# The opening of the shared experts: order of TensorE's steps, of GpSimd's gathers and of ScalarE's casts

## The chip, the cores and the metric

The kernel runs on one core of a Trainium2 chip. The metric is the device time of one execution in microseconds (us), as the median of several runs. Inside the core, TensorE (PE) multiplies matrices, VectorE (DVE), ScalarE (ACT) and GpSimd (POOL) work on tiles of 128 rows, SyncE (SP) issues transfers, and the engines run side by side and wait for each other through semaphores only.

## The reference, cut to what matters

The program is two blocks of cross-attention and mixture of experts over `x` of 4 x 512 tokens with 512 features. The change lies where block 0 ends and the feed-forward part of block 1 begins. What is computed there:

```
x = x + tanh(g_ffn[0]) * mixture0(layernorm(x))            # 2 of 8 experts per token
# block 1, attention: one summary row per batch element
x = x + tanh(g_xattn[1]) * (layernorm(layernorm(x) + summary) * gamma + beta)
# block 1, feed-forward: on flat = layernorm(x)
h   = silu(flat @ Sg) * (flat @ Su)                        # 2 shared experts, 512 wide each
out = h @ Sd  +  4 of 64 routed experts per token
x = x + tanh(g_ffn[1]) * out
```

## The kernel before, in words

The kernel is a sequence of blocks: attention of block 0, `mixture0` (8 experts), `middle` (the end of mixture 0, attention of block 1, routing, and the shared experts), `experts` (64 routed experts) and `finish`. Tokens are handled as 16 tiles of 128; each batch element is a group of four tiles. `middle` is written out by hand: each engine has its own list of steps, executed strictly in the order in which they stand. The change is in the opening of `middle`, the work on group 0 (tiles 0 to 3) before TensorE can start on the shared experts.

For each tile of group 0, in this order:

- GpSimd **gathers** two expert rows per token by indirect DMA into `y0` (`gather(0, ...)`, line 1226), two gathers a tile, eight in all.
- ScalarE makes two diagonal matrices of mixing weights (`diagonals`, 1428).
- TensorE sums `x` and the two weighted rows into a PSUM bank (`mixed(j)`, 1304 and 1306: three 128x512 fp32 products). The banks are `pU[0], pU[1], pC, pU[0]`, so tile 3 has the bank of tile 0, and `mixed(3)` waits for `x3_ready` of tile 0.
- TensorE spreads the summary row of each batch element over 128 rows (`summary_row(b)`, 1295), and ScalarE copies it from its bank (`summary_rows`, 1435). The four rows use banks that the transposes and the first chunks need later, so `transposed(0, 0)` waits for all four copies.
- VectorE takes statistics of the bank, GpSimd raises the variance to the power -1/2 (`inverse_std`, 1215), VectorE makes `z` from the bank (`mix_in`, 1639) and signals `y_made`; statistics of `z` follow, and `z` is scaled by gamma (`attend_to`, 1651).
- TensorE adds the scaled beta into the same bank (`with_beta(j)`, 1314), after `y_made`; VectorE then forms the new `x` from `z` and that bank (`take_in`, 1660), which waits for `with_beta`. Statistics again, and `lnf` holds scale and bias of the last layernorm.
- ScalarE writes the normalised tile (`flat_tile`, 1439), TensorE transposes it (1324), ScalarE copies the transpose twice (`turn`, 1445 and 1446), VectorE takes the low part (`keep`, 1623, signal `fT_kept`), and TensorE starts the shared experts' first products (`shared.up`, 2079) when tiles 0 and 1 are kept. Tiles 2 and 3 go the same way behind them.

Weights are split into a high and a low part. ScalarE casts a half of a weight to the high part (`first_part`, 1418, 128x2048), VectorE subtracts to get the low part (`split`, 1182). `SPLITS` lists four such pieces: two of the up weights `Su`, in SBUF since `mixture0`, and two of the gate weights `Sg`, which SP loads (line 1799) when tile 1's gathers have landed. Two splits stand on VectorE's list inside `mix_in(0)`, the third between `take_in(0)` and `keep(0)`, the fourth after `mix_in(2)`.

GpSimd's list begins with one iota and three memsets (`power` is an operand of `inverse_std`; the others are used later by routing), a drain, a wait for the zeroed tables, and the eight gathers.

The lists of TensorE and ScalarE at this place, before the change:

```
summary_row(0); mixed(0); mixed(1); summary_row(1); mixed(2)
summary_row(2); summary_row(3); with_beta(0); with_beta(1)
mixed(3); transposed(0, 0); transposed(0, 1)
---
summary_rows(range(B)); act.wait_ge(gate_loaded, 16 * NSH)
first_part(SPLITS[NSH:]); flat_tile(0, 0..1); turn(0, 0..1)
```

Of the kernel before, what the change touches and what calls it, by code (L numbers as in the profile page):

```python
# [14 lines left out]
P = 128  # L15
B, SEQ, D = 4, 512, 512
TILES = B * SEQ // P
TPB = SEQ // P
DB = D // P
# [3 lines left out]
NSH, HSH = 2, 512  # L23
# [1037 lines left out]
def middle(nc, A, T):  # L1061
# [4 lines left out]
    with c:  # L1066
# [30 lines left out]
        ve, power = sb("ve1", [P, TPB]), sb("power", [P, TPB])  # L1097
# [105 lines left out]

        @block.gpsimd
        def _(pool):
            nc.gpsimd.iota(tokens[:], [[P, TILES]], base=0, channel_multiplier=1)
            nc.gpsimd.memset(T["stage_all"][:, NSH * DB * HSH:], 0.0)
            nc.gpsimd.memset(power[:], -0.5)
            nc.gpsimd.memset(chosen[:], 0.0)
            pool.drain()  # L1210

            def inverse_std(k, a=0, z_=TPB):

                pool.wait_ge(var_ready, k + 1)
                nc.gpsimd.tensor_tensor(rstd[:, a:z_], ve[:, a:z_], power[:, a:z_], ALU.pow).then_inc(rstd_ready, 1)

            pool.wait_ge(T["s_zero1"], 16 * (ZERO_CHUNKS + SUMS * E0 + 1))
            def gather(n, tiles):

                for j in tiles:  # L1220
                    if n == 1:
                        pool.wait_ge(x2_full, j + 1)
                    elif n > 1:
                        pool.wait_ge(x2_ready, TPB * (n - 2) + j + 1)
                    for k in range(2):
                        nc.gpsimd.indirect_dma_start(
                            y0[:, j, k, :], None, T["ytab0"],
                            bass.IndirectOffsetOnAxis(take0[:, n * TPB + j, k:k + 1], 0)).then_inc(gathered[j], 16)

            def dispatch(g, tiles):  # L1230
                pool.wait_ge(slot_ready, g + 1)
                for j in tiles:
                    for k in range(TOP1):

                        nc.gpsimd.indirect_dma_start(  # L1235
                            T["tab1"], bass.IndirectOffsetOnAxis(slot1[:, j, k:k + 1], 0), flat[:, j, :], None,
                            bounds_check=E1 * CAP1 - 1, oob_is_err=False).then_inc(scattered, 16)

            def sum_up(n):

                inverse_std(stat(n - 1, 0))
                for j in range(TPB):
                    if n == 1 and j == 0:
                        pool.wait_ge(summary_ready, B)
                    pool.wait_ge(z_ready, (n - 1) * TPB + j + 1)
                    nc.gpsimd.tensor_tensor(z[:, j, :], z[:, j, :], summary[:, n, :], ALU.add).then_inc(y_ready, 1)
                for j in range(TPB):
                    nc.gpsimd.tensor_tensor(x_sb[:, n * TPB + j, :], x_sb[:, n * TPB + j, :], beta[:],
                                            ALU.add).then_inc(xb_ready, 1)
                inverse_std(stat(n - 1, 1))  # L1250

            def keep_low(n):

                inverse_std(stat(n - 1, 2))
                for j in range(TPB):

                    pool.wait_ge(fT_ready, TPB * n + j + 1)
                    cols = slice(j * P, j * P + P)
                    nc.gpsimd.tensor_tensor(flat_lo[:, :, cols], flatTt[:, j], flat_hi[:, :, cols],
                                            ALU.subtract).then_inc(fT_kept, 1)  # L1260

            gather(0, range(TPB))
            for k in range(3):
                inverse_std(first_stat(0, k), 0, 2)
            gather(1, (0, 1))
            inverse_std(first_stat(2, 0), 2, 4)
            gather(1, (2,))
            inverse_std(first_stat(2, 1), 2, 4)
            gather(1, (3,))
            inverse_std(first_stat(2, 2), 2, 4)  # L1270
            pool.wait_ge(beta_ready, 1)
            sum_up(1)
            dispatch(0, range(TPB))
            keep_low(1)
            for n in range(2, B):
                gather(n, range(TPB))
                dispatch(n - 1, (0, 1))
                sum_up(n)
                dispatch(n - 1, (2, 3))
                keep_low(n)  # L1280
            dispatch(B - 1, range(TPB))
            pool.wait_ge(scattered, 16 * TILES * TOP1)

        @block.tensor
        def _(pe):
# [5 lines left out]
            def summary_row(b):  # L1291

                if b == 0:
                    pe.wait_ge(srow_ready, 1)
                nc.tensor.matmul(row_bank[b][:], ident[0:B, b:b + 1].broadcast_to([B, P]), srow,
                                 start=True, stop=True).then_inc(rows_full, 1)

            def mixed(j):

                pe.wait_ge(diag_ready, j + 1)  # L1300
                pe.wait_ge(gathered[j], 16 * 2)
                if j == 3:
                    pe.wait_ge(x3_ready, 1)
                nc.tensor.matmul(x2_bank[j][:], ident[:], x_sb[:, j, :], start=True, stop=False)
                for k in range(2):
                    last = nc.tensor.matmul(x2_bank[j][:], diag[:, 2 * j + k, :], y0[:, j, k, :], start=False, stop=(k == 1))
                last.then_inc(x2_full, 1)

            def with_beta(j):

                pe.wait_ge(y_made, j + 1)
                if j == 0:
                    pe.wait_ge(beta_ready, 1)
                nc.tensor.matmul(x2_bank[j][:], ident[:], beta[:], start=False, stop=True,
                                 skip_group_check=True).then_inc(x2b_full, 1)
# [32 lines left out]

            def first_steps():

                summary_row(0)
                mixed(0)
                mixed(1)
                summary_row(1)
                mixed(2)
                summary_row(2)
                summary_row(3)
                with_beta(0)
                with_beta(1)
                mixed(3)  # L1360
                pe.wait_ge(small_loaded, 80)
                transposed(0, 0)
                transposed(0, 1)
# [43 lines left out]
        def _(act):  # L1407
# [23 lines left out]
            def summary_rows(bs):  # L1431

                for b in bs:
                    act.wait_ge(rows_full, b + 1)
                    nc.scalar.copy(summary[:, b, :], row_bank[b][:]).then_inc(summary_ready, 1)
# [17 lines left out]
            first_part(SPLITS[1:2])  # L1453
            diagonals(2)
            diagonals(3)
            summary_rows(range(B))
            act.wait_ge(gate_loaded, 16 * NSH)
            first_part(SPLITS[NSH:])
            for j in range(2):
                act.wait_ge(lnf_ready, j + 1)  # L1460
                flat_tile(0, j)
            for j in range(2):
                turn(0, j)

            def step(g):
                for half, cols in halves(g):
# [677 lines left out]
```

## Time and profile before

| | us |
|---|---|
| median of 3 runs | 1182.45 |
| the 3 runs | 1184.02, 1178.94, 1182.45 |
| the profiled execution, its own time | 1178.42 |
| its span | 1176.7 |
| TensorE busy in the span | 1045.8 (89%) |
| VectorE, ScalarE, GpSimd busy | 675.2, 480.4, 552.2 |

The span is the time between the first and the last recorded instruction; the profiled execution took 1.7 us more than its span. `middle` starts at 550.2 us of the span. A line of a timeline gives the start, the duration, the engine, the source line, the operation and its tiles, how many instructions were merged, and in brackets how long the engine had idled before and what ended that. PSUM tiles are all called `bank`. `w_sd` is also the memory of the diagonals and of the summary row, `stage_up` that of `z` and of the transposed tiles, so these names stand in the rows for them. A 128x512 fp32 product leaves two records.

### The profile page before, as it was taken

The numbers are of one execution on the slowest core, as the hardware profiler recorded it, in microseconds if no ns is written. First come the engines' busy times: TensorE is split into PE (matmuls) and PEld (weight loads), VectorE is DVE, ScalarE is ACT, GpSimd is POOL, SyncE is SP. The second block draws the span as 40 slices with busy tenths as digits, with TensorE's granted clock in tenths as the row PEclk, the third lists the DMA queues.
The fourth block names the chain that finished last, engine by engine and source line by source line (L and its number), as shares of the span: only waits on it lengthen the run. The fifth ranks groups of instructions, "written<-read, shape, count | busy, mean of one in ns | idle before, by whom it ended". The sixth has DMA issues, their size and how long they took to land. (4 is left out here: it accounts for less than half of the span.)

```text
span 1176.7 us, 18454 instructions
## 1 busy us (share of the span) xinstructions
PE 1045.8 (89%) x5324; PEld 735.5 (63%) x5324; DVE 675.2 (57%) x1558; ACT 480.4 (41%) x835; POOL 552.2 (47%) x517
## 2 busy tenths in 40 slices
PE   3999999999879999997798799999998999999920
PEld 2555555555437777774498377586687777787710
DVE  4677777776458888884677256265312333343426
ACT  2465565564338888886322121222212222222200
POOL 4344544644426666666415557446151344333530
PEclk9999999999989999998899899999998999999965
DMA  9976555773534333333610131130029999999639
GB/s 294 345 235 204 169 181 203 252 252 99 197 134 168 103 105 107 107 108 105 217 34 27 75 102 37 41 122 13 27 83 328 362 342 301 279 323 344 146 89 361
DMA packets 133243, 206.54 MB, mean 176 GB/s; under 512 B 36743, under 2 KB 44935, under 8 KB 133178
## 3 DMA queue, kind: packets, MB, share of 16 engines
q1 hardware_dynamic: 113274, 172.72, 43.4%
q0 software_dynamic: 19616, 32.50, 10.1%
q8 instruction: 32, 0.52, 0.2%
q10 hardware_dynamic: 288, 0.52, 0.1%
q14 instruction: 33, 0.27, 0.1%
HBM read 137.56 MB, written 87.03 MB: 191 GB/s over the span
## 5 line engine op out<-in xcount | busy, mean ns | idle before, releaser
L1922 POOL DMA_INDIRECT sums<-summary,m_token x64 | 99.2, 1550 | 161.2 <-DVE summary L1996 86.2
L906 POOL TENSOR_TENSOR m_down_lo<-wo,m_down_hi 128x512 fp32r<-128x512 f32 x80 | 133.0, 1682 | 79.7 <-ACT m_down_hi L1001 79.7
L514 PE MATMUL bank<-win,vT 128*128 128x512 f32 x256 | 124.2, 598 | 0.0
L604 ACT ACTIVATE win<-bank 128x512 f32<-128x512 f32 x128 | 69.5, 595 | 109.4 <-PE bank L506 109.2
L674 DVE TENSOR_REDUCE negmax<-bank 128x1 bf16<-128x512 f32 x128 | 87.0, 679 | 43.3 <-PE bank L521 43.0
L1015 DVE TENSOR_TENSOR m_up_lo<-w,m_up_hi 128x1024 fp32r<-128x1024 f32 x80 | 98.3, 1230 | 12.0 <-ACT m_up_hi L973 10.9
L521 PE MATMUL bank<-k_hi,q_parts 128*128 128x512 f32 x128 | 76.8, 600 | 17.0 <-DVE negmax L674 13.4
L1945 PE MATMUL bank<-y,m_w 128*128 128x128 f32 x736 | 89.7, 275 | 0.0
L1235 POOL DMA_INDIRECT tab<-stage_up,slot x64 | 66.3, 1036 | 49.2 <-DVE slot L1570 31.0
L1945 PEld LDWEIGHTS bank<-y,m_w 128*128 128x128 f32 x736 | 86.4, 193 | 0.5 <-issue 0.5
L2100 PE MATMUL bank<-w_sd,stage_gate 128*128 128x512 f32 x192 | 84.9, 598 | 0.3 <-DVE stage_gate L2090 0.3
L2086 ACT ACTIVATE sh_gate_a<-bank 128x512 f32<-128x512 f32 (+1 forms) x40 | 20.5, 513 | 149.9 <-PE bank L2079 149.9
L1970 ACT COPY y<-bank 128x512 f32<-128x512 f32 x64 | 37.5, 586 | 102.5 <-PE bank L1937 99.4
L1996 DVE TENSOR_SCALAR summary<-bank,m_weight 128x512 f32<-128x512 f32 x64 | 48.1, 751 | 54.2 <-DMA sums<-summary,m_token 29.5
L2079 PE MATMUL bank<-flat_hi,w_hi 128*128 128x512 f32 (+1 forms) x320 | 74.8, 357 | 3.0 <-DVE flat_lo L1623 1.9
L404 POOL DMA_INDIRECT tab<-xn,slot x32 | 32.8, 1024 | 94.4 <-DVE slot L708 89.5
L2079 PE MATMUL bank<-flat_lo,w_hi 128*128 128x512 f32 (+1 forms) x320 | 73.0, 351 | 0.0
L2079 PE MATMUL bank<-flat_hi,w_lo 128*128 128x512 f32 (+1 forms) x320 | 72.4, 349 | 0.0
L927 PE MATMUL bank<-m_up_hi,m_xT_hi 128*128 128x512 f32 x160 | 69.6, 435 | 1.9 <-DVE m_up_lo L1015 1.6
L1983 DVE TENSOR_TENSOR m_gh<-m_gh,bank 128x128 f32<-128x128 f32 x64 | 18.4, 287 | 90.0 <-ACT m_gh L1974 90.0
L514 PEld LDWEIGHTS bank<-win,vT 128*128 128x128 f32 x256 | 47.0, 190 | 26.1 <-issue 15.3
L2100 PEld LDWEIGHTS bank<-w_sd,stage_gate 128*128 128x128 f32 x192 | 36.4, 193 | 42.8 <-issue 42.6
(282 smaller groups left out, 2383.8 us busy)
## 6 DMA issues: line engine op xcount, KB each, us to landing
tab<-zeros SPq DMA_DIRECT2D x16, 1056.0 KB
m_w<-in_L_ffn_Wg SPq DMA_DIRECT2D x46, 256.0 KB, 5.3
m_w<-in_L_ffn_Wu SPq DMA_DIRECT2D x46, 256.0 KB, 5.9
m_w<-in_L_ffn_Wd SPq DMA_DIRECT2D x46, 256.0 KB, 6.2
m_x<-tab SPq DMA_DIRECT2D x40, 256.0 KB, 2.6
ytab<-m_y SPq DMA_DIRECT2D x40, 256.0 KB, 2.0
stage_up<-tab SPq DMA_DIRECT2D x32, 264.0 KB, 7.4
m_x<-tab SPq DMA_DIRECT2D x32, 264.0 KB, 5.7
```

Source lines behind the costliest of these rows:

```text
L514: nc.tensor.matmul(pO[s * 2 + h][:], vT[:, s, sb_, h:h + 2, :].rearrange("p a c -> p (a c)"), probs[:, sb_ % 2, h, :], start=(sb_ == 0), s ...
L521: nc.tensor.matmul(pM[:], q_parts[:, s, h, t * P:t * P + P], k_hi[:, s, h, :], start=True, stop=True).then_inc(pm_full, 1)
L604: nc.scalar.activation(probs[:, b % 2, h, :], pS[h][:], ACT.Exp, scale=1.0 / HEAD).then_inc(p_ready, 1)
L674: nc.vector.tensor_reduce(negmax[:, s, m:m + 1], pM[:], AX.X, ALU.max, negate=True).then_inc(pm_read, 1)
L906: nc.gpsimd.tensor_tensor(dn_lo[:, m, :], row(wo0, e * MB + m), dn_hi[:, m, :], ALU.subtract).then_inc(dn_lo_ready, 1)
L927: last = nc.tensor.matmul(pH[s][:], x[:, s, d, :], w[:, d, :], start=(d == 0 and part == 0), stop=(d == DB - 1 and part == 2))
L1015: nc.vector.tensor_tensor(up_lo[:, at, :], blocks(w01, e * DB + half * HALF, HALF), up_hi[:, at, :], ALU.subtract).then_inc(up_lo_ready, 1)
L1235: nc.gpsimd.indirect_dma_start(T["tab1"], bass.IndirectOffsetOnAxis(slot1[:, j, k:k + 1], 0), flat[:, j, :], None, bounds_check=E1 * CAP1 ...
L1922: nc.gpsimd.indirect_dma_start(T["sums1"][e % SUMS], bass.IndirectOffsetOnAxis(token[:, e % META:e % META + 1], 0), y[:, e % RING, :], Non ...
L1945: last = nc.tensor.matmul(pH[s][:, k * CAP1:(k + 1) * CAP1], w[:, b, :], xT[:, s, b, :], start=(b == 0), stop=(b == DB - 1))
L2079: last = nc.tensor.matmul(out, w[:, k, s, wc], x[:, d, cols], start=(d == 0 and part == 0), stop=(d == DB - 1 and part == 2))
L2100: last = nc.tensor.matmul(pY[j][:], self.h[:, n, j * P:j * P + P], sd[:, s, b, :], start=(n == 0), stop=(n == self.CHUNKS - 1))
```

## The change

TensorE's list: `mixed(0)` goes before `summary_row(0)`, and `with_beta(0)` and `with_beta(1)` go before `mixed(2)`. GpSimd's list: the iota, the memsets and their drain go behind the eight gathers of group 0. ScalarE's list: the first gate cast goes between the copies of summary rows 0 and 1 and those of rows 2 and 3; the second gate cast goes behind both turns.

```diff
         @block.gpsimd
-            nc.gpsimd.iota(tokens[:], [[P, TILES]], base=0, channel_multiplier=1)
-            nc.gpsimd.memset(T["stage_all"][:, NSH * DB * HSH:], 0.0)
-            nc.gpsimd.memset(power[:], -0.5)
-            nc.gpsimd.memset(chosen[:], 0.0)
-            pool.drain()
...
             gather(0, range(TPB))
+            nc.gpsimd.memset(power[:], -0.5)
+            nc.gpsimd.iota(tokens[:], [[P, TILES]], base=0, channel_multiplier=1)
+            nc.gpsimd.memset(T["stage_all"][:, NSH * DB * HSH:], 0.0)
+            nc.gpsimd.memset(chosen[:], 0.0)
+            pool.drain()
             for k in range(3):
                 inverse_std(first_stat(0, k), 0, 2)
...
             def first_steps():
+                mixed(0)
                 summary_row(0)
-                mixed(0)
                 mixed(1)
                 summary_row(1)
+                with_beta(0)
+                with_beta(1)
                 mixed(2)
                 summary_row(2)
                 summary_row(3)
-                with_beta(0)
-                with_beta(1)
                 mixed(3)
...
-            summary_rows(range(B))
+            summary_rows(range(2))
             act.wait_ge(gate_loaded, 16 * NSH)
-            first_part(SPLITS[NSH:])
+            first_part(SPLITS[NSH:NSH + 1])
+            summary_rows(range(2, B))
             for j in range(2):
                 act.wait_ge(lnf_ready, j + 1)
                 flat_tile(0, j)
             for j in range(2):
                 turn(0, j)
+            first_part(SPLITS[NSH + 1:])
```

## Rows read from the trace of the kernel before

**Rows 1.** Busy time by stretch: length, PE, PEld, DVE, ACT, POOL, clock, DMA share, GB/s

```profile
548.00:584.00 36.00, 26.00 (x54) 9.15 (x55) 20.64 (x38) 18.26 (x25) 17.61 (x19) 0.83 0.57 187
```

**Rows 2.** Timeline of PE, 556 to 584 us: start, duration, instruction [idle before]

```profile
556.88 1.12 PE L1295 MATMUL bank<-w_sd,ident 4*128 4x512 f32 x2 [1.45 <-DVE w_sd L1515]
557.93 1.12 PE L1304 MATMUL bank<-x_sb,ident 128*128 128x512 f32 x2
...
560.61 1.02 PE L1304 MATMUL bank<-x_sb,ident 128*128 128x512 f32 x2
...
563.27 1.12 PE L1295 MATMUL bank<-w_sd,ident 4*128 4x512 f32 x2
566.85 1.80 PE L1304 MATMUL bank<-x_sb,ident 128*128 128x512 f32 x2 [2.45 <-DMA y<-ytab,take]
...
571.29 1.98 PE L1295 MATMUL bank<-w_sd,ident 4*128 4x512 f32 x4
573.20 1.98 PE L1314 MATMUL bank<-beta,ident 128*128 128x512 f32 x4
...
579.90 1.63 PE L1324 MATMUL bank<-ident,stage_up 128*128 128x128 f32 x8 [1.83 <-issue]
583.42 1.22 PE L2079 MATMUL bank<-flat_hi,w_hi 128*128 128x256 f32 x4 [1.89 <-DVE flat_lo L1623]
```

**Rows 3.** Timeline of DVE, 557 to 583 us

```profile
557.42 2.29 DVE L1182 TENSOR_TENSOR w_lo<-stage_up,w_hi 128x2048 fp32r<-128x2048 f32 x1 [0.20 <-DMA y<-ytab,take]
560.81 0.70 DVE L1635 BATCH_NORM_STATS2 bn<-bank 128x6 f32<-128x512 f32 x1 [1.09 <-PE bank L1306]
561.42 2.28 DVE L1182 TENSOR_TENSOR w_lo<-stage_up,w_hi 128x2048 fp32r<-128x2048 f32 x1
563.61 0.69 DVE L1635 BATCH_NORM_STATS2 bn<-bank 128x6 f32<-128x512 f32 x1
...
565.73 1.41 DVE L1639 SCALAR_TENSOR_TENSOR stage_up<-bank,rstd,summary 128x512 f32<-128x512 f32 x2 [0.85 <-POOL rstd L1215]
...
570.04 1.41 DVE L1651 SCALAR_TENSOR_TENSOR stage_up<-stage_up,mv,gamma 128x512 f32<-128x512 f32 x2
574.36 1.61 DVE L1660 SCALAR_TENSOR_TENSOR x_sb<-stage_up,rstd,bank 128x512 f32<-128x512 f32 x2 [2.92 <-PE bank L1314]
...
578.87 2.31 DVE L1182 TENSOR_TENSOR w_lo<-stage_gate,w_hi 128x2048 fp32r<-128x2048 f32 x1
581.67 0.69 DVE L1623 TENSOR_TENSOR flat_lo<-stage_up,flat_hi 128x512 fp32r<-128x512 f32 x1 [0.49 <-ACT stage_up L1446]
```

**Rows 4.** Timeline of POOL, 550 to 565 us

```profile
550.48 0.15 POOL L1209 MEMSET chosen<- 128x64 bf16 x1
551.51 1.00 POOL L1226 DMA_INDIRECT y<-ytab,take  x1 [0.88 <-issue]
...
558.35 2.19 POOL L1226 DMA_INDIRECT y<-ytab,take  x1 [0.30 <-issue]
...
562.10 2.42 POOL L1226 DMA_INDIRECT y<-ytab,take  x1 [0.30 <-issue]
564.96 0.73 POOL L1215 TENSOR_TENSOR rstd<-ve,power 128x2 f32<-128x2 f32 x1 [0.43 <-DVE ve L1587]
```

**Rows 5.** Timeline of ACT, 573 to 589 us

```profile
573.78 3.70 ACT L1418 CAST w_hi<-stage_gate 128x2048 fp32r<-128x2048 f32 x2
578.99 1.52 ACT L1439 ACTIVATE stage_up<-x_sb,lnf 128x512 f32<-128x512 f32 x2 [1.50 <-DVE lnf L1667]
588.42 0.38 ACT L2086 ACTIVATE sh_gate_a<-bank 128x256 f32<-128x256 f32 x1 [4.48 <-PE bank L2079]
```

**Rows 6.** Busy time in half microseconds: where the granted clock fell and rose

```profile
567.00:567.50 0.50, 0.50 (x1) 0.12 (x2) 0.41 (x2) 0.00 (x0) 0.00 (x0) 0.60 1.03 397
...
570.50:571.00 0.50, 0.50 (x2) 0.00 (x0) 0.50 (x2) 0.00 (x0) 0.00 (x0) 0.98 0.00 0
```

**Rows 7.** Timeline of PE, first product that waits inside the chunks

```profile
599.85 0.74 PE L2079 MATMUL bank<-flat_hi,w_hi 128*128 128x256 f32 x4 [1.12 <-DVE stage_gate L2090]
```

## The prediction

> **What bounds the kernel now.** I read the busy time by stretch first, then the timelines of the four engines over the opening of `middle`, then the clock. In the 36 us around the opening TensorE is busy 26.0, VectorE 20.6, ScalarE 18.3 and GpSimd 17.6 [rows 1]: no engine fills it, so a chain of dependencies sets its length, and the end to look for is the first product of the shared experts at 583.42, which waits for VectorE's `keep` [rows 2]. Followed back from there: `keep(0)` at 581.67 waits for ScalarE's `turn` [rows 3]; ScalarE starts the flat tiles at 578.99 after 1.50 idle, for `lnf` [rows 5]; `lnf` comes from `take_in(0)`, which started at 574.36 after 2.92 us in which VectorE had nothing but TensorE's `with_beta` to wait for [rows 3]. `with_beta` ran at 573.20 although its `z` was there since about 567.1 (565.73 + 1.41), because `mixed(2)` (from 566.85, after 2.45 idle for tile 2's gather) and rows 2 and 3 (from 571.29) stood ahead of it on TensorE's list [rows 2, 3]. Before that the chain is: the second statistics at 563.61, GpSimd's power at 564.96, `z` at 565.73, `attend_to` at 570.04 to 571.45 [rows 3, 4].
>
> From `keep` on VectorE works nearly without a gap, and the first product that waits in the chunks, at 599.85, waits again for VectorE [rows 7]. So what counts is how far `keep(0)` moves; a faster TensorE in chunk 0 would not. Nothing after the opening is timed against anything but these signals: the loads of expert weights, routing and the later groups all wait for products of this chain, so I carry the move to the end one for one. That is the main assumption.
>
> **The parts of the change.**
>
> *with_beta ahead of mixed(2).* Removed: VectorE's wait of 2.92. `attend_to(0)` ends at 571.45; with a gap of 0.1 as between its neighbours `take_in(0)` starts at 571.55 instead of 574.36: 2.8 us gained. `with_beta(0)` can start when the first `z` is written, about 566.45, and costs at full clock half of the pair's pitch (573.20 to 575.25, cut by `mixed(3)`: 2.05), 1.0, or 2.0 at half clock: done by 568.5, 3.0 us before it is needed. The new wait is TensorE's, for `y_made`; behind it stand `mixed(2)`, rows 2 and 3, `mixed(3)`, and the transposes. What is late next is this queue. From 566.45: with_beta pair 2.05, `mixed(2)` 2.66 (pitch 560.61 to 563.27), rows 2 and 3 1.91 (571.29 to 573.20), `mixed(3)` 2.82 (the end of the idle at 579.90 less 1.83 is 578.07, less the pair's end at 575.25) [rows 2]: 9.44, so ready for the transposes at 575.9. At the moved time the first flat tile is written at 578.99 + 0.76 - 2.8 = 576.95 [rows 5]: TensorE is there 1.0 earlier, if its clock stays up. The bank of `mixed(3)` is free when `take_in` of tile 0 is through, about 572.4, and `mixed(3)` comes at 573.1.
>
> *The clock.* The granted clock fell 0.3 us after the idle of 2.45 before `mixed(2)`, and was back at 570.5 after 3.4 us of dense work [rows 6]; 0.50 is 1.2 GHz, 1.00 is 2.4. That made `mixed(2)` last 4.44 (566.85 to 571.29) instead of 2.66: 1.8 us. In the changed kernel TensorE idles from about 564.3 to 566.45, 2.1 us, so the same fall is likely, now in `with_beta` and `mixed(2)`. Then the queue ends at 577.7, 0.75 after the first flat tile. In the old order the turn began at 580.5, when the two flat tiles were written (578.99 + 1.52) and about 0.6 after the transposes began; at the moved times ScalarE is free at 577.7 and TensorE's first transposed tile is there at 577.7 + 0.8 (half of 1.63) = 578.5 [rows 2, 5]. Cost between 0 (no fall) and 0.8; I take 0.5, nearer the upper end, since shorter idles, 1.83 and 1.89 in a row, also left TensorE slow: four products of 256 columns took 1.22 at 583.42 and 0.74 at 599.85 [rows 2, 7].
>
> *mixed(0) ahead of summary_row(0).* Tile 0's bank is full 1.05 earlier (the pitch of row 0, 556.88 to 557.93), so the first statistics start at about 559.8, not 560.81 after 1.09 idle, and the second split ends at about 562.6 [rows 2, 3]. But the second statistics need `mixed(1)`, and the sum of TensorE's work before it is the same, so it starts at 563.4 instead of 563.61: 0.2 gained. More only if TensorE can start before 556.88, that is if tile 0's gathers, which released VectorE at 557.42 [rows 3], land earlier.
>
> *Gathers first.* The first gather started at 551.51 after 0.88 idle, of which 0.30 stands before every gather; the iota and the memsets began 0.2 before 550.48 [rows 4]. So it moves up by 0.3 to 1.0. With it tile 0 lands by 556.4 to 557.0, and TensorE starts up to 0.5 earlier. Against this, the five instructions and the drain (at most 0.37 + 0.58) now stand between the last gather and GpSimd's first power, which had 0.43 idle before it [rows 4]. And the gathers do not simply shift. Those at 558.35 and 562.10 took 2.19 and 2.42 instead of 1.00; both began inside a split on VectorE (557.42 to 559.71, 561.42 to 563.70) and ended 0.83 and 0.82 after it [rows 3, 4]. The new second split runs from about 560.4 to 562.6. If two gathers are left at that time, the last ends at 564.6 and the power starts at 565.0 to 565.6, as late as 0.6 after the old time; if one is left, it ends at 563.4 and the power starts when the variance is there, 0.2 to 0.7 earlier. Range -0.6 to +0.7; I take 0.
>
> On this the Trainium skill (SBUF — State Buffer, "SBUF: two separate sides") has a rule that speaks against the change: a VectorE instruction with two SBUF inputs and a GpSimd instruction that reads SBUF exclude each other for their whole length, and a locked-out GpSimd cannot write descriptors. The stretched gathers of this trace agree. By the rule alone the early gathers win nothing once the splits begin; by the rows alone the same, which is why the step is put at 0.
>
> *The gate cast split in two.* The casts ran at 573.78, behind row 3's copy, 1.88 each, 3.70 together [rows 5]. The weights had landed by 570.5, where the DMA share is 0.00 [rows 6]. Now the first cast runs at about 570 to 572, ahead of rows 2 and 3, which TensorE fills at 571.1 to 574.8; the copies, 0.6 each, are done by 575.5, before `lnf` at 576.2: nothing lost. The second cast, 1.9, goes behind the turns, from about 580 to 582; its reader is the fourth split, some 5 us after `keep(1)`, and the first silu, which had 4.48 idle before 588.42 [rows 5], covers it and the table load. Cost 0; without that cover 1.9. The third split on VectorE, 2.31 from `lnf`, ends before the turn as now (581.18 against 581.67) [rows 3].
>
> **Sum.** 2.8 + 0 - 0.5 = 2.3 us earlier `keep`. The profiled execution took 1178.42: it would take 1176.1. It is 4.0 under the median of the three runs; the four executions together average 1180.95. From that average the forecast is 1178.7, which I take; it is 3.8 under the median shown, of which 1.5 is spread between executions.
>
> **Rivals.**
>
> *The clock stays up, or an earlier start comes through.* 2.8 + 0.7 and, where a slow stretch elsewhere in the chunks falls differently, up to 1.8 more: 3.5 to 5.3, about 1176. For it: the idle shrinks from 2.45 to 2.1. Against: the idles of 1.83 and 1.89 that were enough once [rows 2]. 0.17.
>
> *The gain is given back.* The gathers and memsets make the power late by 0.6, TensorE's queue costs 0.8, and the end of `middle` is held by something that does not move: 0 to 1.4 left, about 1180.5. For it: the lock on gathers; against: the signals below all come from this chain. 0.25.
>
> *TensorE's queue takes the place of the wait, slower.* If the clock fell at 566.5 and stayed at 1.2 GHz to the transposes, the queue of 9.44 would take near 18 us and end at 584: 4 us after the old 579.90, so 3 to 4 us slower, about 1184. It decides from the point where the low clock lasts over 4 us beyond the 3.4 seen (each us of it costs half a us; the queue's end passes 579.90). Against: the clock came back under the same products [rows 6]. 0.05. The ScalarE copy of this mechanism, rows 2 and 3 and the flat tiles behind a late load of `Sg`, needs a landing 6 us later than in this trace; in the 0.05.
>
> *The change does not do what it says:* `take_in` would still wait for `with_beta`. Excluded by the 3.0 us in hand unless `z` itself is late; in the second rival.
>
> **How the numbers follow.** Forecast (gain 1.5 to 3.5) 0.53; the rivals 0.17, 0.25, 0.05. Range: gains from -1.5 to 5.3 and a spread of the median of +-2 around the average: 1174.5 to 1184. 0.5% (5.9 us) is about what a measurement of this kernel tells from no change. A forecast of 1178.7 lies inside 1176.5 to 1188.4; with the spread a fifth of the forecast and half of the first rival come out under 1176.5, and a little of the rest: 0.23 faster. The third rival's tail gives 0.04 slower. 0.73 remain.
>
> **What would show it.** In the changed trace: `take_in` with next to no idle before it; `with_beta` some 7 us earlier; `keep(0)` about 2.3 earlier against the start of `middle`; the power after the eighth gather with less than 0.43 idle; the clock low within `with_beta` and `mixed(2)`; the copies of rows 2 and 3 done before `lnf`. Wrong would be: transposes that wait for `mixed(3)` by over 1 us, a fourth split that waits for its cast, or chunk times that shift by another amount than `keep`.

## The result, and the profile after

The changed kernel took 1185.0 us, median of 22 runs (1181.8 to 1189.2); the kernel before, run beside it, 1181.5, median of 22 (1176.4 to 1189.2). The ratio is 1.0032 with a 95% interval of 1.0019 to 1.0045: 3.8 us slower (2.2 to 5.3). 2.3 us faster was forecast.

The profiled execution of the changed kernel had a span of 1185.0. Its opening began 3.7 us later than that of before, in code that both kernels share, so all positions below count from **the opening's start**, the first state product of TensorE (550.27 in before, 553.99 here). From there `keep(0)` comes at 34.3 instead of 31.4: 2.9 later.

The timeline of GpSimd in the changed kernel, the last three of the eight gathers, a memset behind them, and the first power:

```profile
561.00 3.99 POOL L1220 DMA_INDIRECT y<-ytab,take  x1 [0.30 <-issue]
565.29 2.86 POOL L1220 DMA_INDIRECT y<-ytab,take  x1 [0.30 <-issue]
568.46 0.95 POOL L1220 DMA_INDIRECT y<-ytab,take  x1 [0.30 <-issue]
...
569.63 0.17 POOL L1260 MEMSET chosen<- 128x64 bf16 x1
573.15 0.73 POOL L1209 TENSOR_TENSOR rstd<-ve,power 128x2 f32<-128x2 f32 x1 [3.35 <-issue]
```

The drain is an instruction of GpSimd's queue; the view by its source line gives its length and its start:

```profile
L1261 POOLq DRAIN  x1: 15104/15104/15104, 557.9 to 557.9; - x1
```

It entered at 557.9, while gathers were still being issued, and ended at 573.0, 3.2 us after the last memset. The power followed 0.15 later. In before the idle ahead of this power was 0.43, for the variance [rows 4]. What moved in the core's DMA engines meanwhile, in the view of busy time by stretch (the last three columns are the granted clock, the DMA share and GB/s):

```profile
571.00:572.00 1.00, 0.00 (x0) 0.00 (x0) 0.00 (x0) 0.59 (x1) 0.00 (x0) 1.00 0.80 324
572.00:573.00 1.00, 0.00 (x0) 0.00 (x0) 0.00 (x0) 1.00 (x1) 0.00 (x0) 1.00 0.04 16
```

In the view of the DMA queues the last packet of the gathers' queue falls before 572.4, and that of the queue of `Sg` before 571.2. So the drain's end lies 0.6 behind the end of the gathers' transfers. VectorE, with the lines that answer to [rows 3]:

```profile
564.45 0.70 DVE L1636 BATCH_NORM_STATS2 bn<-bank 128x6 f32<-128x512 f32 x1 [0.28 <-PE bank L1305]
...
568.27 0.70 DVE L1636 BATCH_NORM_STATS2 bn<-bank 128x6 f32<-128x512 f32 x1 [0.93 <-PE bank L1305]
...
573.92 1.41 DVE L1640 SCALAR_TENSOR_TENSOR stage_up<-bank,rstd,summary 128x512 f32<-128x512 f32 x2 [4.37 <-POOL rstd L1209]
...
579.71 1.41 DVE L1661 SCALAR_TENSOR_TENSOR x_sb<-stage_up,rstd,bank 128x512 f32<-128x512 f32 x2
...
588.25 0.69 DVE L1624 TENSOR_TENSOR flat_lo<-stage_up,flat_hi 128x512 fp32r<-128x512 f32 x1 [1.93 <-ACT stage_up L1445]
```

`take_in(0)` no longer waits, as forecast, but `z` waits 4.37 for the power. TensorE, against [rows 2]:

```profile
561.60 1.10 PE L1303 MATMUL bank<-x_sb,ident 128*128 128x512 f32 x2 [1.18 <-DMA y<-ytab,take]
...
574.73 3.78 PE L1313 MATMUL bank<-beta,ident 128*128 128x512 f32 x4 [5.44 <-DVE stage_up L1640]
578.30 1.92 PE L1303 MATMUL bank<-x_sb,ident 128*128 128x512 f32 x2
...
581.92 1.98 PE L1294 MATMUL bank<-w_sd,ident 4*128 4x512 f32 x4
...
586.51 1.04 PE L1323 MATMUL bank<-ident,stage_up 128*128 128x128 f32 x8
```

It idled 5.44 for `z`, ran the pair at a granted clock of 0.50, 1.2 GHz (3.78, not 1.98), and reached the transposes at 586.5, 2.1 after the first flat tile was begun. ScalarE, against [rows 5]:

```profile
584.42 1.52 ACT L1438 ACTIVATE stage_up<-x_sb,lnf 128x512 f32<-128x512 f32 x2
587.15 0.58 ACT L1444 CAST flat_hi<-bank 128x512 fp32r<-128x512 f32 x1 [1.21 <-PE bank L1323]
```

The turn waited 1.21 for them.

Against before, the 2.9 at `keep(0)` add up so: the power is 4.5 later, 1.0 of it because the variance was and 3.5 by the drain; 2.8 come back from the wait for `with_beta` that is gone, and 0.2 because `take_in` took 1.41 and not 1.61; ScalarE starts the flat tile 0.3 later behind `lnf`, since it still copies row 3; the turn's wait adds 1.15.

### The profile page after: what moved, and what is told of

It is laid out like the page before. It is cut to its first block and busy times, and to the rows that moved or that the text cites. A ratio compares the mean times of both kernels' runs of the same rounds, so it can differ in the third digit from the quotient of the medians.

```text
span 1185.0 us, 18454 instructions
## 1 busy us (share of the span) xinstructions
PE 1053.3 (89%) x5324; PEld 738.7 (62%) x5324; DVE 675.7 (57%) x1558; ACT 480.1 (41%) x835; POOL 553.0 (47%) x517
## 5 line engine op out<-in xcount | busy, mean ns | idle before, releaser
L521 PE MATMUL bank<-k_hi,q_parts 128*128 128x512 f32 x128 | 76.5, 598 | 18.2 <-DVE negmax L674 14.2
L404 POOL DMA_INDIRECT tab<-xn,slot x32 | 32.7, 1023 | 96.0 <-DVE slot L708 91.1
L521 PEld LDWEIGHTS bank<-k_hi,q_parts 128*128 128x128 f32 x128 | 25.0, 195 | 62.3 <-DVE negmax L674 50.5
```

Of the source, the lines that this page charges most:

```text
L521: nc.tensor.matmul(pM[:], q_parts[:, s, h, t * P:t * P + P], k_hi[:, s, h, :], start=True, stop=True).then_inc(pm_full, 1)
```

## The experiments

Times are positions from the opening's start in each kernel's own profiled execution; ratios are to the kernel before on the same chip. In the table "first of TensorE" is the step that stands first, row 0 or `mixed(0)`, and "2nd st." the second tile's statistics. A profiled execution is one of those timed, and not the median one: of `power first` the second time, `power by VectorE` and `power first, row first` it was the slowest of the twelve.

| kernel | first of TensorE | 2nd st. | power | take_in(0) | keep(0) | ratio (95%) |
|---|---|---|---|---|---|---|
| before, four profiles | row | 13.3, 13.5, 16.3, 17.6 | 14.7, 14.9, 17.7, 19.0 | 24.1, 24.1, 24.2, 25.5 | 31.4, 31.4, 31.3, 32.6 | 1 |
| changed, two profiles | mixed | 14.3, 14.0 | 19.2, 19.1 | 25.7, 25.7 | 34.3, 34.5 | 1.0032 (1.0019 to 1.0045) |
| gathers back | mixed | 14.6 | 15.9 | 22.5 | 29.7 | 0.9988 (0.9969 to 1.0006) |
| gathers only | row | 16.3 | 19.1 | 25.6 | 32.7 | 1.0012 (0.9995 to 1.0030) |
| drain late | mixed | 13.8 | 19.0 | 25.6 | 33.0 | 1.0016 (0.9999 to 1.0033) |
| power first | mixed | 14.4, 13.9 | 15.8, 15.3 | 22.3, 21.8 | 29.5, 30.6 | 0.9969 (0.9950 to 0.9988), 0.9986 (0.9965 to 1.0007) |
| gathers only, Sg late | row | 18.2 | 19.5 | 26.1 | 33.2 | 1.0026 (1.0003 to 1.0049) |
| power first, row first | row | 18.9 | 20.2 | 26.8 | 34.3 | 1.0017 (1.0000 to 1.0034) |
| beta only | row | 16.6 | 17.9 | 24.5 | 34.5 | 1.0004 (0.9983 to 1.0025) |
| power first, casts back | mixed | 14.4 | 15.8 | 22.3 | 32.3 | 0.9999 (0.9980 to 1.0018) |
| power by VectorE | mixed | 14.2 | 15.5 | 22.1 | 29.6 | 0.9981 (0.9961 to 1.0001) |
| mixed first only | mixed | 14.6 | 15.9 | 22.5 | 29.6 | 0.9995 (0.9973 to 1.0017) |

**Which part of the change is it?** First GpSimd's list put back as it was, in the changed kernel (diff against the changed kernel):

```diff
+            nc.gpsimd.iota(tokens[:], [[P, TILES]], base=0, channel_multiplier=1)
+            nc.gpsimd.memset(T["stage_all"][:, NSH * DB * HSH:], 0.0)
+            nc.gpsimd.memset(power[:], -0.5)
+            nc.gpsimd.memset(chosen[:], 0.0)
+            pool.drain()
...
             gather(0, range(TPB))
-            nc.gpsimd.memset(power[:], -0.5)
-            nc.gpsimd.iota(tokens[:], [[P, TILES]], base=0, channel_multiplier=1)
-            nc.gpsimd.memset(T["stage_all"][:, NSH * DB * HSH:], 0.0)
-            nc.gpsimd.memset(chosen[:], 0.0)
-            pool.drain()
```

> The changed kernel with GpSimd's list as it was before: iota, memsets and drain ahead of the eight gathers. TensorE's and ScalarE's lists stay changed. Theory D (the drain behind the gathers does it): in the changed kernel GpSimd is idle 3.35 us between its last memset and the first power. Without that drain the power starts when the variance is there, at most 0.5 after it; take_in(0) starts with under 0.1 idle, some 22.9 us after the opening's start against 24.1 before and 25.7 changed; TensorE's queue costs 0.8 to 1.2 of the 2.8 won, so the kernel is 1.5 to 2 us faster than before (ratio 0.998 to 0.999). Rival Q (TensorE's new order does it: the queue behind with_beta and the low clock): the loss stays, ratio 1.002 to 1.004.

Measured 0.9988 (0.9969 to 1.0006), `keep(0)` at 29.7, and the power waits for nothing but the variance:

```profile
569.67 0.73 POOL L1215 TENSOR_TENSOR rstd<-ve,power 128x2 f32<-128x2 f32 x1 [3.76 <-DVE ve L1589]
```

Its interval and that of the changed kernel don't meet, and the two kernels differ in GpSimd's list alone. The loss sits there. Then that list alone, changed on the kernel before (the diff above, reversed):

> The kernel before with GpSimd's list alone changed (gathers first, then memsets, iota and drain). Theory D: the first power is some 4.4 us later against the opening's start; z, too; but with_beta had 2.9 us of wait behind mixed(2) to give, so take_in(0) and keep(0) come about 1.6 us later: ratio 1.001 to 1.002, and less slow than the changed kernel, since here mixed(2) and rows 2 and 3 run while z is late. Rival Q: GpSimd's change costs nothing: ratio 1.000, power with under 1 us of idle before it.

Measured 1.0012, the power at 19.1, as theory D said, with the idle below ahead of it; `keep(0)` at 32.7, against 31.3 to 32.6. Only the last 1.4 of the 6.15 are the drain's: the variance itself came at 17.6 here. The ratio's interval holds 1.

```profile
573.78 0.73 POOL L1209 TENSOR_TENSOR rstd<-ve,power 128x2 f32<-128x2 f32 x1 [6.15 <-issue]
```

**The drain, or what else moved?** TensorE's and ScalarE's lists changed, iota and memsets ahead of the gathers, only the drain behind (GpSimd's list, against before):

```diff
             nc.gpsimd.memset(chosen[:], 0.0)
-            pool.drain()
...
             gather(0, range(TPB))
+            pool.drain()
```

> TensorE's and ScalarE's lists changed; on GpSimd iota and memsets stay ahead of the gathers as before, and only the drain stands behind the gathers. Theory D: as slow as the changed kernel (ratio to before 1.002 to 1.004), idle of about 3 us before the first power, though no memset stands there. Rival M (the early gathers disturb the small loads, or the memsets behind the gathers take the time): as fast as the kernel with GpSimd's list back, 0.998 to 0.999.

Measured 1.0016, the power at 19.0, though the variance was there at 15.1:

```profile
571.47 0.73 POOL L1214 TENSOR_TENSOR rstd<-ve,power 128x2 f32<-128x2 f32 x1 [4.08 <-issue]
```

This kernel and `gathers back` differ in the drain's place alone and ran on the same chip: the power is at 19.0 and not at 15.9, `keep(0)` at 33.0 and not at 29.7, while their ratios' intervals overlap. The half of rival M about the memsets falls: none stands there. Its other half, the early gathers, falls with the next kernel, where they are as early (0.9) and the power waits for the variance alone. The other way round, the drain out of the way (against the changed kernel):

```diff
+            nc.gpsimd.memset(power[:], -0.5)
+            pool.drain()
...
             gather(0, range(TPB))
-            nc.gpsimd.memset(power[:], -0.5)
-            nc.gpsimd.iota(tokens[:], [[P, TILES]], base=0, channel_multiplier=1)
-            nc.gpsimd.memset(T["stage_all"][:, NSH * DB * HSH:], 0.0)
-            nc.gpsimd.memset(chosen[:], 0.0)
-            pool.drain()
             for k in range(3):
                 inverse_std(first_stat(0, k), 0, 2)
+            nc.gpsimd.iota(tokens[:], [[P, TILES]], base=0, channel_multiplier=1)
+            nc.gpsimd.memset(T["stage_all"][:, NSH * DB * HSH:], 0.0)
+            nc.gpsimd.memset(chosen[:], 0.0)
+            pool.drain()
```

> The changed kernel, but the memset of power and a drain stand ahead of the gathers, and the iota, the two other memsets and their drain behind the third inverse_std, when the eight gathers have landed some microseconds ago. Theory D with the drain waiting for landed transfers: the second drain takes under 0.6 us here, the first power waits for the variance alone, and the kernel is 1.5 to 2.5 us faster than before (0.998 to 0.999). If the drain costs a fixed 3.3 us after any gather, the first gathers of group 1 start over 3 us after the third power, which delays no chain at once but the power of tiles 2 and 3: ratio 1.001 or more. Rival Q: 1.002 to 1.004.

Measured 0.9969 (0.9950 to 0.9988): faster than before, and the fastest of the study. The second drain now stands 11 us behind the last gather's issue, with the DMA share at 0.00 from 580 to 583. It was 1.74 in the queue and ended 0.7 after the last memset, where under 0.6 was expected, and it left 1.47 idle ahead of the next gather, of which 0.30 stand there anyway. This costs a little: group 1's gathers now end so late that the power of tile 2 comes behind them, and `z` of tile 2 waits 1.42 for it, where it waits 0.84 with the gathers back.

```profile
571.47 0.73 POOL L1212 TENSOR_TENSOR rstd<-ve,power 128x2 f32<-128x2 f32 x1 [0.21 <-DVE ve L1590]
...
583.91 1.60 POOL L1223 DMA_INDIRECT y<-ytab,take  x1 [1.47 <-issue]
```

**What does the drain wait for?** Three kernels with it have the power at 19.0 to 19.2, whether the last gather ended at 15.4, 12.5 or 15.0. So it is no fixed time after the last gather's issue. `Sg` later, on the kernel with GpSimd's list alone changed:

```diff
-            sp.wait_ge(gathered[1], 16 * 2)
+            sp.wait_ge(gathered[3], 16 * 2)
             for s in range(NSH):
                 sp.dma_start(stage[0][:, s].rearrange("p (b h) -> p b h", b=DB),
```

> The kernel before with GpSimd's list changed (gathers, memsets, iota, drain), and SP's load of Sg moved behind the landing of tile 3's gathers instead of tile 1's. Theory L (the drain behind the gathers waits until what GpSimd has issued has landed, and the 2 MB of Sg in the same engines delay that): the last gathers land about 4 to 5 us after their start, at 16 to 17 us from the opening's start, and the first power starts within 1 us of that, 1.5 to 3 us earlier than the 19.0 seen in three kernels with this drain. Rival F (a fixed time of the drain after the gathers began, near 15 us from its entry into the queue): the power stays at 19.0. The gate casts come later than before by some 5 us, so the time itself need not improve: ratio 1.000 to 1.004.

The drain, and the stretches at its end (opening's start 553.42):

```profile
L1261 POOLq DRAIN  x1: 11816/11816/11816, 557.4 to 557.4; - x1
```

```profile
568.00:569.00 1.00, 1.00 (x2) 0.34 (x1) 0.32 (x1) 0.00 (x0) 0.00 (x0) 0.50 0.25 98
569.00:570.00 1.00, 1.00 (x3) 0.38 (x2) 1.00 (x2) 0.00 (x0) 0.00 (x0) 0.92 0.07 16
```

It ended at 569.2, which is 15.8 from the start, when the gathers had landed (SP issued `Sg` at 568.8, on tile 3's signal). It was 11.8 us in the queue instead of 15.0 to 15.1: rival F falls, theory L holds. The expectation was wrong in one point: the power still started at 19.5, because here the variance came that late. The time did not improve (1.0026).

A rival is left that was not on record: that the drain waits for every transfer of the core, those of `Sg` too. The trace of the kernel with the gathers only excludes it. Its drain:

```profile
L1261 POOLq DRAIN  x1: 15019/15019/15019, 558.7 to 558.7; - x1
```

It ended at 573.7. The DMA queues (packets, MB, share of 16 engines) from 572 to 573 and from 573 to 574; q0 is that of the gathers, which alone moved packets from 565 to 567.5 in the kernel with `Sg` late, when nothing else was under way:

```profile
q1 hardware_dynamic: 126, 0.24, 62.4%
q0 software_dynamic: 31, 0.07, 16.7%
...
q1 hardware_dynamic: 52, 0.09, 24.0%
```

From 573.0 on only the queue of `Sg` moved packets, until 574.2, and the drain ended amid them. In all five executions with a drain behind the gathers it ended 0.6 to 0.7 us after the last packet of the gathers' queue.

On the length of that landing the Trainium skill (DMA: Bandwidth & Descriptors, "Queues, rings and completion order") says that a DMA engine takes packets from its queues in turn. The runs agree: with `Sg` beside them the last gather needed about 7.4 us from its start to the drain's end (566.3 to 573.7, gathers only), without it 3.8 (565.4 to 569.2).

**Is mixed(0) ahead of row 0 worth anything?** Row 0 first again, in the kernel with power first:

```diff
-                mixed(0)
                 summary_row(0)
+                mixed(0)
```

> The kernel with power's memset and drain first, but summary_row(0) ahead of mixed(0) as before. Theory R (tile 0's gathers land after the summary row is ready, so the row filled the wait for them; mixed(0) first pushes the row between mixed(0) and mixed(1)): second statistics at 13.4 to 13.6 us from the opening's start against 14.4 to 14.6, everything after it 0.9 to 1.0 earlier, ratio 0.996. Rival (the gathers land first, the order does not matter, as the sum of the prediction had it): second statistics unchanged or 0.2 later, ratio 0.997.

Both expectations missed the size and the side: the second statistics moved from 14.4 to 18.9, not to 13.5, and the ratio from 0.9969 to 1.0017. TensorE:

```profile
562.80 1.84 PE L1296 MATMUL bank<-w_sd,ident 4*128 4x512 f32 x2 [2.41 <-DVE w_sd L1518]
564.57 2.08 PE L1305 MATMUL bank<-x_sb,ident 128*128 128x512 f32 x2
566.44 3.61 PE L1307 MATMUL bank<-y,w_sd 128*128 128x512 f32 x4
```

Row 0 waited for the summary row, which waited for the small loads, 2.2 us later here than in the profile of before (8.1 from the start, not 5.9). Behind that idle the granted clock fell: 0.54 from 563 to 564 and 0.50 (1.2 GHz) from 564 to 569, so most of row 0 and all of `mixed(0)` ran at 1.2 GHz. Over all profiles of the study the second statistics stand at 13.8 to 14.6 in the nine executions with `mixed(0)` first, and at 13.3 to 18.9 in the eight with row 0 first. Part of that spread is the small loads' own. Where VectorE took up the summary row at the same time, 7.1 to 7.2, they stand at 14.4 with `mixed(0)` first (`power first`, `casts back`) and at 16.3 with row 0 first (the third profile of before, `gathers only`). In the ratio the order's worth is less sure: 1.0017 (1.0000 to 1.0034) does not meet the first interval of `power first`, but it overlaps the second.

**with_beta alone**, on the kernel before:

```diff
                 summary_row(1)
+                with_beta(0)
+                with_beta(1)
                 mixed(2)
                 summary_row(2)
                 summary_row(3)
-                with_beta(0)
-                with_beta(1)
```

> The kernel before with one edit: with_beta(0) and with_beta(1) ahead of mixed(2). take_in(0) starts at about 21.3 us from the opening's start against 24.1. If the gate casts behind rows 2 and 3 (3.7 us on ScalarE) are what comes next, the rows are copied at 23.5 to 25.5, the casts end at 27.3 to 29.2, the flat tile starts there against 28.7 before: 1.4 earlier to 0.5 later, ratio 0.999 to 1.0005. If the casts do not matter, keep(0) is 2.3 earlier, ratio 0.998.

Measured 1.0004, `keep(0)` at 34.5, 1.9 to 3.2 us later than in the profiles of before. `take_in(0)` came at 24.5 and not at 21.3, because the second statistics stood at 16.6 in this execution, and the flat tile at 31.8, later than both branches had it. ScalarE:

```profile
582.41 0.59 ACT L1435 COPY summary<-bank 128x512 f32<-128x512 f32 x1 [0.27 <-PE bank L1295]
582.90 3.70 ACT L1418 CAST w_hi<-stage_gate 128x2048 fp32r<-128x2048 f32 x2
586.50 1.52 ACT L1439 ACTIVATE stage_up<-x_sb,lnf 128x512 f32<-128x512 f32 x2
```

`mixed(2)` and the rows are pushed back behind `with_beta`, the casts behind the rows with them, and the flat tile follows the casts without idle. The second branch of the expectation (casts do not matter) falls. The same from the other side, ScalarE's old list in the kernel with power first (against that kernel):

```diff
-            summary_rows(range(2))
+            summary_rows(range(B))
             act.wait_ge(gate_loaded, 16 * NSH)
-            first_part(SPLITS[NSH:NSH + 1])
-            summary_rows(range(2, B))
+            first_part(SPLITS[NSH:])
...
             for j in range(2):
                 turn(0, j)
-            first_part(SPLITS[NSH + 1:])
```

> The kernel with power's memset and drain first, with ScalarE's list as it was before (four row copies, then both gate casts, then the flat tiles). The rows are copied at about 24.4 us from the opening's start, the two casts take 3.8, so the flat tile starts at 28.2 instead of 26.8: 1.4 us slower than with the casts split, ratio to before 0.998 to 0.999. If the split of the casts is worth nothing: 0.997 as with it.

Measured 0.9999, `keep(0)` at 32.3 against 29.5 and 30.6, where 1.4 was expected. ScalarE once more goes from the casts into the flat tile without idle:

```profile
578.79 3.70 ACT L1419 CAST w_hi<-stage_gate 128x2048 fp32r<-128x2048 f32 x2
582.39 1.52 ACT L1440 ACTIVATE stage_up<-x_sb,lnf 128x512 f32<-128x512 f32 x2
```

So at `keep(0)` the split pays for `with_beta`'s new place. The ratios do not tell it: 0.9999 (0.9980 to 1.0018) overlaps both of `power first`.

**Can the gathers still start earlier?** VectorE writes `power` at the head of its list, and GpSimd begins with the gathers (against the kernel with power first):

```diff
         @block.gpsimd
         def _(pool):
-            nc.gpsimd.memset(power[:], -0.5)
-            pool.drain()
...
         @block.vector
         def _(dve):
             nc.vector.tensor_tensor(wtmp[:, 0, :], top0[:, :, 1], top0[:, :, 0], ALU.subtract).then_inc(wexp_ready, 1)
+            nc.vector.memset(power[:], -0.5)
```

> As the kernel with power's memset first, but VectorE sets power at the start of its list, so nothing stands ahead of the gathers on GpSimd. If the landing of tile 0's gathers sets the start of mixed(0): first gather at 0.7 us from the opening's start instead of 0.9, mixed(0) 0.2 to 0.5 earlier than 7.8, ratio to before 0.9965. Rival (the small loads in the same engines set the landing): mixed(0) at 7.6 to 7.9 as before, ratio as for the kernel with power first.

Measured 0.9981 (0.9961 to 1.0001); beside it the kernel with power first, once more:

> The kernel with power's memset first once more, on another chip than the first time perhaps. Theory D: ratio to before 0.996 to 0.999. If the first ratio of 0.9969 was luck: 1.000.

0.9986 (0.9965 to 1.0007). The two can't be told apart, nor either from 0.9969. Nor do the traces show a gain by the earlier start: with the first gather at 0.7, `mixed(0)` starts at 7.5; with it at 0.9, at 7.8 in the first profile and at 7.2 in the second. And `mixed(0)` first as the only edit on the kernel before:

> The kernel before with one edit: mixed(0) ahead of summary_row(0). Prediction's sum: 0.2 us, ratio 1.000. Theory R2 (in most executions the small loads come late, the summary row is ready only at 7.8 to 8.8 us from the opening's start, and the idle ahead of it lets the clock fall, which lengthens mixed(0)): second statistics at 13.8 to 14.6 instead of 16.3 to 18.9 in four kernels with the row first (13.3 in the profile of before); with_beta still waits behind mixed(2), and keep(0) moves by what is left of it, 0.5 to 2: ratio 0.998 to 0.9995.

Its ratio, 0.9995 (0.9973 to 1.0017), tells nothing, but its trace does: `with_beta` stands behind `mixed(2)`, and `take_in(0)` does not wait for it, against the expectation.

```profile
569.00 1.41 DVE L1639 SCALAR_TENSOR_TENSOR stage_up<-bank,rstd,summary 128x512 f32<-128x512 f32 x2 [0.85 <-POOL rstd L1215]
574.79 1.41 DVE L1660 SCALAR_TENSOR_TENSOR x_sb<-stage_up,rstd,bank 128x512 f32<-128x512 f32 x2
```

That put the forecast's main term in question: the wait of 2.92 [rows 3] might belong to one execution. So the kernel before was profiled three times more, and the changed one once.

> The kernel before, profiled once more. Theory S (the wait of 2.9 us for with_beta in the profile of before belongs to that execution: the small loads came early, so the first split began at 7.15 us from the opening's start and locked out tile 2's second gather; in most executions it begins later and locks out a gather of tile 3, which nothing waits for): first split at 7.6 or later, take_in(0) 5.8 us after z, without a wait for with_beta; second statistics at 13.3 to 18.9. Rival: the wait is there in each execution, 8.6 us from z to take_in(0).

> The kernel before, profiled a third time; as for the second: 5.8 us from z to take_in(0) by theory S, 8.6 by the rival.

> The kernel before, profiled a fourth time; as for the second.

> The changed kernel, profiled once more: the power at 19.0 to 19.2 us from the opening's start and take_in(0) 5.8 after z in this execution too, since the drain's end is set by the transfers and not by the clock; keep(0) at 33 to 34.5.

The wait is in two of four executions. Where the small loads came early, it is there (second profile, opening's start 549.19):

```profile
573.26 1.60 DVE L1660 SCALAR_TENSOR_TENSOR x_sb<-stage_up,rstd,bank 128x512 f32<-128x512 f32 x2 [2.74 <-PE bank L1314]
```

Where they came late (third profile, start 551.65), it is not, but the first statistics wait longer for `mixed(0)` on a slow clock:

```profile
565.18 0.70 DVE L1635 BATCH_NORM_STATS2 bn<-bank 128x6 f32<-128x512 f32 x1 [3.08 <-PE bank L1306]
...
575.89 1.41 DVE L1660 SCALAR_TENSOR_TENSOR x_sb<-stage_up,rstd,bank 128x512 f32<-128x512 f32 x2
```

So the second profile misses theory S and the third and fourth agree with it in the wait, but not in its reason. It said that an early first split locks out tile 2's second gather and a later one a gather of tile 3. In the third profile it is again tile 2's second gather that is stretched, to 3.71, and `mixed(2)` waited only 0.24 for it. What differs there is that the slow stretch of TensorE lies in `mixed(0)` and not in `mixed(2)`; why it moves with the small loads is read from four traces, not tested.

Both end alike: `keep(0)` at 31.4, 31.4, 31.3 and, with the latest loads, 32.6. "In most executions" of theory S is not shown; "not in all" is. The changed kernel repeats itself, as expected: the power at 19.2 and 19.1, `keep(0)` at 34.3 and 34.5. Its mean is 2.7 above that of before (31.7); the ratio says 3.8 (2.2 to 5.3).

## Why the prediction was wrong

- **The step that failed: "the five instructions and the drain (at most 0.37 + 0.58)"**. The 0.58 was the price of a drain with nothing outstanding, read from the list's head [rows 4] and carried to a place behind eight gathers. There it waits for their landing: 3.35 us of idle, and the power at 19.2 instead of 14.7 in the profiled executions (1.0 of it because the variance itself was later), where the range of this step ended at 0.6 later. Shown by the pair that differs in the drain's place alone (`drain late`, `gathers back`), by the kernels with the drain out of the way, and by the one in which `Sg` was moved. The landing itself was not in the sum at all: only the issue times of the gathers were.
- **"with_beta ahead of mixed(2): 2.8 us."** The wait went, as said, but the power's lateness came on the same chain. And it is not worth 2.8 in every execution: in two of four of before there is no such wait. One edit, `mixed(0)` first, reaches 29.6 at `keep(0)` without moving `with_beta`, and `gathers back`, which moves it as well, 29.7. Alone the step lost 2.8 at `keep(0)` against the mean of before, by the casts. A trace of one execution can't tell a wait of the program from one of that execution.
- **"mixed(0) ahead of summary_row(0): 0.2."** Too small for most executions: 13.8 to 14.6 against 13.3 to 18.9. It makes TensorE start with a step that does not need the small loads. In the profile the forecast went by, these were at their earliest, so there the order even cost about 1 us (14.3 against 13.3). The prediction's own rows pointed to this: it let `mixed(0)` start at 556.88, while tile 0's gathers released VectorE at 557.42, and in the changed kernel `mixed(0)` did wait for them.
- **"Gathers first."** The first gather moved from 1.24 to 0.71. Among the kernels that begin with `mixed(0)`, that step starts at 7.9 in the two with the old gathers (gathers back, mixed first only) and at 7.1 to 7.8, mean 7.5, in the seven executions with the first gather at 0.7 to 0.9. So 0.4 was perhaps there to win, inside the 0.5 allowed; two executions on one side are few, and the ratios are too wide to show it.
- **The lock on gathers** was right. The changed kernel's gather at 561.00 ran through VectorE's scaling of beta and first split (561.89 to 564.16) and ended at 564.99, 0.83 after; it took 3.99. By the Trainium skill (SBUF — State Buffer, "SBUF: two separate sides") the side that holds the shared port keeps it for a whole instruction; two VectorE instructions in a row give two of them. The gather itself had begun first, at 561.00, and did not hold up VectorE, whose split took its usual 2.27: from that side the trace does not show the rule. The stretched gathers (3.99 and the next, 2.86) also pushed the last gather back, for which the drain waited. Whether this cost anything is open: in `gathers only` the last gather ended 2.9 earlier and the power came at the same place, with `Sg` still under way.
- **The clock** (0 to 0.8, taken as 0.5): right in kind, with the upper end short. The idle ahead of `with_beta` was 5.44, not 2.1; the pair took 3.78, and the turn waited 1.21 for the transposes. Elsewhere with `with_beta` moved, that wait was 0 and 1.21 in the two profiles of `power first` and 0.20 in `gathers back`, so it goes by the execution as well. The sign that the prediction named, transposes behind `mixed(3)` by over 1 us, came true: they began 1.3 after the first flat tile was written.
- **The gate cast split**, put at 0, is worth 1.7 to 2.8 at `keep(0)` once `with_beta` is moved (32.3 against 29.5 and 30.6); it was right that it costs nothing.
- **The carrying to the end** holds roughly. The kernels' ratios follow `keep(0)`: 29.5 to 30.6 goes with 0.997 to 0.9995, 32.3 to 33.2 with 1.000 to 1.003, 34.3 to 34.5 with 1.0004 to 1.003. It is no more exact than the intervals.
- **The rival on the other side** named TensorE's queue and gave 0.05. The loss came by GpSimd's drain; the prediction had no rival for it. "The gain is given back" had its place, with 0.6 for a power that came 4.5 later.

The best order found is power first, 0.9969 and 0.9986. The second interval holds 1, so a gain of 0.1 to 0.3% over before is likely rather than shown. Against the changed kernel it is some 0.5% (1.0032 to about 0.998), and neither interval meets that of the changed kernel.

## What to carry to other kernels

A drain is priced by what stands before it. Behind indirect DMAs it waited until they had landed, and a large load beside them lengthened that (to 19.0 from the opening's start, 15.8 without it). Set up constants and drain ahead of the first gather, or let another engine write them. Before a wait of a few microseconds is counted as a gain, profile the same kernel two or three times; the wait may trade places with another from one execution to the next.

## What the runs showed of the hardware that was not expected

- GpSimd's drain behind the gathers ended 0.6 to 0.7 us after the last packet of the gathers' queue, in five executions of four kernels (15.1 twice, 15.0, 15.0 and, without `Sg` in the way, 11.8 us in the queue), also where the queue of `Sg` moved on for 0.5 us more. With nothing under way it took 0.36 at the head of the list in before, and 1.74 behind a power, the iota and two memsets in `power first`, where it ended 0.7 after the last memset.
- The five small loads of the opening, issued within 3 us of its start, released VectorE at 5.9, 6.0, 7.2 and 8.5 from the start in four executions of one kernel.
- The same state product at the opening's start took TensorE 4.9 to 6.5 us, by where the granted clock rose from 0.50 to 1.00 within it: 2.7 us after its start in the second profile of before (4.93), 5.7 us after it in the third (6.39).
